# A graph propagation in dense counts: the last source tile's products of two target tiles in the two halves of the array's rows

## The reference, cut to what matters

```python
deg  = segment_sum(ones, dst);  dinv = rsqrt(max(deg, 1)) where deg > 0 else 0
norm = (dinv[src] * dinv[dst])[:, None]
def prop(h):
    return segment_sum(h[src] * norm, dst, num_segments=n)
out = gamma[0] * x
h = x
for k in range(10):
    h = prop(h)
    out = out + gamma[k + 1] * h
x = layernorm(x + out)
```

## Time and profile before

| | |
|---|---|
| median of 3 runs | 2363.64 us (2362.68 to 2366.68) |
| the profiled execution | 2366.91 us, of which 2365.2 us between the first and the last instruction |
| TensorE busy, matmul | 2159.4 us (91%), 22505 matmuls |
| TensorE busy, weight load | 1795.4 us (76%) |
| VectorE busy | 1832.0 us (77%) |
| ScalarE busy | 1162.6 us (49%) |
| propagation (first L891 to the end of its last `turn`) | 440.8 to 981.4 us |
| mean granted TensorE clock | 0.96 of full speed |

### The profile page before, as it was taken

One profiled execution on the slowest core, in us unless ns is written; L12 is line 12 of the kernel. 1 busy time (PEld: TensorE's weight loads), 2 busy tenths in 40 slices (PEclk: granted clock), 3 DMA queues, 4 the chain that ended last, 5 costly groups with the idle time before them and its releaser, 6 DMA issues. The chain is left out here.

```text
span 2365.2 us, 63175 instructions
## 1 busy us (share of the span) xinstructions
PE 2159.4 (91%) x22505; PEld 1795.4 (76%) x22506; DVE 1832.0 (77%) x2687; ACT 1162.6 (49%) x2789; POOL 879.4 (37%) x1062
## 2 busy tenths in 40 slices
PE   2888888799999999888999978999999999999897
PEld 2777777799999999622222225999996799999787
DVE  8899988765655566578999976988886788887446
ACT  1888888432332333388999966231322432230323
POOL 3444444000000000067888832555552455555000
PEclk8999999899999999989999979999998999999899
DMA  2344444200100000242222224223224322222800
GB/s 67 153 166 165 164 166 159 106 30 30 43 30 30 29 29 15 65 108 57 57 57 59 57 97 159 84 73 88 75 60 127 139 74 77 85 75 45 343 11 22
DMA packets 94785, 205.64 MB, mean 87 GB/s; under 512 B 21718, under 2 KB 61270, under 8 KB 94450
## 3 DMA queue, kind: packets, MB, share of 16 engines
q1 hardware_dynamic: 81458, 182.46, 22.3%
q0 software_dynamic: 13120, 20.18, 4.3%
HBM read 116.99 MB, written 84.76 MB: 85 GB/s over the span
## 5 line engine op out<-in xcount | busy, mean ns | idle before, releaser
L1873 PE MATMUL l_bank<-tab,mask 128*128 128x192 f16 x7600 | 636.3, 247 | 8.3 <-PEq L1704 3.5
L1873 PEld LDWEIGHTS l_bank<-tab,mask 128*128 128x128 f16 x7600 | 629.5, 98 | 10.8 <-issue 10.2
L1459 DVE TENSOR_SCALAR mask<-code 128x1600 int32<-128x1600 int32 x304 | 546.7, 1816 | 91.6 <-PE l_bank L1873 82.7
L1849 POOL DMA_INDIRECT ggot<-table_dram,gidx x408 | 386.2, 947 | 264.7 <-PE l_bank L1873 204.0
L1356 DVE TENSOR_TENSOR pr<-ex,count_copy 128x1568 f32<-128x1568 f32 x200 | 351.0, 1786 | 24.7 <-POOL ex L1255 12.8
L1346 ACT ACTIVATE ex<-score_pair,poss 128x784 f32<-128x784 f32 x400 | 344.0, 910 | 30.0 <-PE score_pair L1294 18.6
L1255 POOL TENSOR_SCALAR ex<-ex 128x1568 f32<-128x1568 f32 x200 | 298.5, 1493 | 78.2 <-ACT ex L1346 71.1
L891 PE MATMUL sums<-onehots,ct 128*128 128x192 f16 x3125 | 266.5, 250 | 11.6 <-issue 7.3
L891 PEld LDWEIGHTS sums<-onehots,ct 128*128 128x128 f16 x3125 | 263.9, 99 | 14.1 <-issue 7.9
L891 PE MATMUL sums<-u,ct 128*128 128x192 f16 x3125 | 259.1, 246 | 0.0
L891 PEld LDWEIGHTS sums<-u,ct 128*128 128x128 f16 x3125 | 258.0, 98 | 0.0
(11 more groups left out here) (344 smaller groups left out, 2873.0 us busy)
## 6 DMA issues: line engine op xcount, KB each, us to landing
code<-code_dram SPq DMA_DIRECT2D x38, 800.0 KB
code_dram<-flat SPq DMA_DIRECT2D x100, 200.0 KB, 1.9
ct_dram<-ct SPq DMA_DIRECT2D x25, 800.0 KB, 3.5
c_dram<-flat SPq DMA_DIRECT2D x25, 800.0 KB, 3.4
ct_again<-ct_dram SPq DMA_DIRECT2D x25, 800.0 KB, 17.3
cring<-c_dram SPq DMA_DIRECT2D x200, 98.0 KB, 1.9
table_dram<-tab SPq DMA_DIRECT2D x50, 384.0 KB, 2.3
flat<-code_dram SPq DMA_DIRECT2D x19, 800.0 KB, 4.4
```

The lines of the kernel that those rows point to most:

```text
L1459: e.tensor_scalar(turned.rearrange("p (s q d) -> p s q d", q=NQ, d=DQ // 2), words.rearrange("p (q s d) -> p s q d", q=NQ, d=DQ // 2), abs ...
L1849: e.indirect_dma_start(ggot[:, k, j, :], None, table_dram[:, :], bass.IndirectOffsetOnAxis(ap=gidx[:, k, j:j + 1], axis=0)).then_inc(s_ggo ...
L1873: mm = e.matmul(acc[k][:, 0:2 * D], mask[:, r % MR, s, :], tab[:, s, r, :], start=(r == 0 and s == 0), stop=(r == R - 1 and s == NT - 1))
```

## The change

In every step, target tile t now runs its 24 full products only. Behind the 24 of an odd t come two half products: source tile 24 for t - 1 from partitions 0 to 63, and source tile 24 for t from partitions 64 to 127. They use the upper and the lower half of the array's rows and write two different PSUM banks. The last tile, t = 24, has no partner and does its half alone. For this the rows 0 to 63 of `ct[:, :, 24, :]` are copied once to rows 64 to 127 by a DMA on SyncE's queue (ahead of the code loads), and the values of tile 24 are copied to partitions 64 to 127 by VectorE: once for the first step, then at the end of each step but the last. An even tile's `s_sum` is signalled behind its successor's 24 products. TensorE's wait for tile 24's values moves from the end of t = 0 to the end of t = 1; there it waits for the DMA too, and so does ScalarE before its first tile.

```diff
@@ rows_split, counting phase
                         c(e.tensor_tensor(u[0][:, ts, 1, :], val[:, ts, :], u[0][:, ts, 0, :], ALU.subtract))
+                        if ts.stop == NT:
+                            c(e.tensor_copy(u[0][HP:P, NT - 1, :, :], u[0][0:HP, NT - 1, :, :]))
@@ semaphores of the phase
+            s_twin, s_last = sem("l0_twin"), sem("l0_last")
+            assert N - (NT - 1) * P <= HP and NT % 2 == 1
@@ SyncE, behind its waits and ahead of load_code
+                    e.dma_start(ct[HP:P, :, NT - 1, :], ct[0:HP, :, NT - 1, :]).then_inc(s_twin, 16)
@@ TensorE, step
                             e.wait_ge(s_free, n + 1)
-                            for s in range(NT):
+                            for s in range(NT - 1):
                                 if t == 0:
                                     e.wait_ge(s_u, n + (s + 1))
-                                mm = e.matmul(sums[t % RS][:, 0:2 * D], ct[:, t, s, :],
-                                              u[par][:, s, :, :].rearrange("p k d -> p (k d)"),
-                                              start=(s == 0), stop=(s == NT - 1))
-                            mm.then_inc(s_sum, 1)
+                                e.matmul(sums[t % RS][:, 0:2 * D], ct[:, t, s, :],
+                                         u[par][:, s, :, :].rearrange("p k d -> p (k d)"),
+                                         start=(s == 0), stop=False)
+                            if t == 1:
+                                e.wait_ge(s_u, first + NT)
+                                e.wait_ge(s_twin, 16)
+                            if t % 2 or t == NT - 1:
+                                for v in range(t - t % 2, t + 1):
+                                    half = slice(v % 2 * HP, v % 2 * HP + HP)
+                                    e.matmul(sums[v % RS][:, 0:2 * D], ct[half, v, NT - 1, :],
+                                             u[par][half, NT - 1, :, :].rearrange("p k d -> p (k d)"),
+                                             start=False, stop=True).then_inc(s_sum, 1)
                             if last and t >= 9 and t % 5 == 4:
                                 turn(t // 5 - 1)
@@ VectorE, tile
-                            e.scalar_tensor_tensor(new[:, t, 1, :], Sb, rdeg[:, t:t + 1], new[:, t, 0, :],
-                                                   ALU.mult, ALU.subtract).then_inc(s_u, 1)
+                            low = e.scalar_tensor_tensor(new[:, t, 1, :], Sb, rdeg[:, t:t + 1], new[:, t, 0, :],
+                                                         ALU.mult, ALU.subtract)
+                            if t < NT - 1:
+                                low.then_inc(s_u, 1)
+                            else:
+                                low.then_inc(s_last, 1)
+                                e.wait_ge(s_last, k + 1)
+                                e.tensor_copy(new[HP:P, t, :, :], new[0:HP, t, :, :]).then_inc(s_u, 1)
```

## The result

The changed kernel takes **2383.05 us** (median of 4 runs, 2380.0 to 2385.2) against 2363.16 for the kernel before (4 runs, 2361.9 to 2366.7): a ratio of 1.0077 with a 95% interval of 1.0062 to 1.0092. By this ratio it is slower by 18.2 us (14.6 to 21.7); the two medians lie 19.9 us apart. The forecast was 2382.7 us, and the forecast case is the one that happened.

What follows compares the result with a forecast made beforehand. TensorE's issue pace was taken as the bound. 18.1 us for ten steps, 0.25 for the copy, 0.3 at turn(1) and 0.5 at the end gave +19.1 us, a median of 2382.7 us, range 2366 to 2392.

Steps and rivals of the forecast that it cites:

- the forecast case: Whole kernel: changes of array shape cost more than side-by-side halves save; 2382.7 us, chance 0.60.
- The bound: Propagation: TensorE's issue pace, one full product every 0.0824 us, bounds the time one for one.
- The drain: TensorE, 26 shape changes a step: each empties the array, 0.0916 us more for a change.
- The first rival: Load behind the 24th product: no drain between full and half rows; 2357 to 2359 us, chance 0.12.
- the cheaper drain: Shape changes: half rows leave sooner or only one direction drains; about 2370.7 us, chance 0.10.
- The fourth: A second cost on top: clock falls to 1.2 GHz more often, or a late DMA; 2398 us, chance 0.05.
- The halves side by side: Each pair's second half product starts 0.015 us behind the first, removing 0.067 us a pair, 8.1 us over 120 pairs.
- The sum: Propagation steps: 12 pairs and tile 24's lone half add 1.81 us a step, 18.1 us over ten steps.
- the single: Tile 24's half product without a partner, once a step: two shape changes and small sums, +0.201 us.
- The copy ahead of the barrier: End of the counting phase: VectorE's copy of tile 24's values counts whole, +0.25 us once.
- The twin DMA: Copy of ct rows ahead of the code loads: 4 us, hidden; upper bound 8 us, leaving 1 to 2 us once.
- The last step: Later tiles delay turn(1) by 0.3 us and the tail at the end by 0.5 us.

Runs made afterwards that it cites:

- e1_full_rows: Changed kernel with the last products of a pair on all 128 rows, both copies going to unread memory; 2365.05 us, 1.0012 of the kernel before.
- e4_each_half: Kernel before with the last source tile's product on rows 0 to 63 in each of 250 tiles, no pairs; 2415.37 us, ratio 1.0229.
- e2_same_half: Changed kernel with both halves of a pair on rows 0 to 63; 2389.74 us, 1.0117 of the kernel before.
- e6_last_full: Changed kernel with tile 24's last product on all 128 rows again; 2379.84 us, 1.0071 of the kernel before.
- e10_before_again: Kernel before, unedited, profiled once more; a single run of 2368.62 us.
- e5_96_rows: Kernel before with the last source tile's product on rows 0 to 95 in each of 250 tiles; 2364.70 us, ratio 1.0013.
- e8_32_rows: Kernel before with the last source tile's product on rows 0 to 31 in each of 250 tiles; 2415.20 us, ratio 1.0223.
- e7_half_stream: Kernel before with all but tile 24 in half-row products, sums not the reference's; 2361.46 us, ratio 0.9999.

## Why the prediction was right, step by step

**The bound.** TensorE's issue pace was read as the bound from the earlier trace rows. It holds: 1.8 us more in the stream of an undisturbed step, ten times, are 18 of the 18.2 us.

**The drain.** This was the step on which all hung, and its evidence was thin for rows: the earlier trace rows shows two cases at the lower clock with a semaphore near. The weight load starts 0.17 us behind the last full product, as worked out from the earlier trace rows, and 0.18 behind the halves, whose recorded time is 0.253 us instead of 0.246. That the price is a wait for the product ahead, and not a fixed price of the change, is seen where the product ahead is longer: behind the 392 columns of L1294 the load starts 1255.15 - 1254.89 = 0.26 us after its start. This is a change of columns; for rows only 192 columns were run. e1_full_rows shows that nothing else costs, e4_each_half the price by itself: 0.21 us for an excursion of two changes, where the prediction had 0.201. The first rival (no drain) and the cheaper drain fall. The fourth, a lower clock more often or a late DMA, falls too: the mean granted clock is 0.962 against 0.960, and between 440.7 and 1000 us TensorE waits for no DMA. The Trainium skill's "up to two times" stands in "TensorEngine Tiling (Array Packing)" under Overview, Theoretical Speedup, and not under Performance Considerations as the prediction has it.

**The halves side by side.** Taken as 0.015 us apart, from the earlier trace rows; at most 0.01 in the trace. 0.005 to 0.01 less, 120 times, is about 1 us that makes up for the longer way out. The outcome was right, but the row behind the 0.015 couldn't show it: L1294's two loads take 0.11 us together while their products start 0.18 apart, and e2_same_half has the same 0.11 with products that run one after the other. The four heads side by side in the columns (0.008 each) were the row that bore on it, and here the size was partly luck.

**The sum.** Pairs of +0.134 us and the single of +0.201 were to make 1.81 us a step. Measured are 1.8 for the step, 0.2 for the single (53.3 against 53.1 in e6_last_full) and so 1.6 / 12 = 0.13 for a pair.

**The copy ahead of the barrier.** 0.25 us were counted. The order of time there, as in the earlier trace rows, with the new DMA and the first pair:

```profile
439.56 0.20 DVE L505 COPY onehots<-onehots 64x192 f16<-64x192 f16 x1
440.27 0.10 POOL L872 MEMSET wmax<- 128x2 f32 x1 [18.18 <-POOLq L420]
...
440.81 0.78 SPq L850 DMA_DIRECT2D ct<-ct  x1
...
447.66 0.26 PE L906 MATMUL sums<-onehots,ct 64*128 64x192 f16 x2
```

The copy takes 0.20 us, and the barrier opens at 440.27 where it did at 440.04 (the same row in the trace of before).

**The twin DMA.** It was taken at 4 us, hidden. Its row in the list of DMA issues between 440 and 446 us (the last number is us from issue to landing):

```profile
ct<-ct SPq DMA_DIRECT2D x1, 400.0 KB, 4.7
```

It landed at 440.8 + 4.7 = 445.5, 2.2 us before the first pair at 447.66 asks for it. The issue of the two code loads behind it took 2.7 us instead of 1.0, which nobody waited for.

**The last step.** 0.3 us were put at turn(1) and 0.5 at the end. Around turn(1):

```profile
964.66 0.26 PE L906 MATMUL sums<-u,ct 64*128 64x192 f16 x2
...
965.80 1.29 DVE L994 TENSOR_SCALAR x<-x,l_st 128x96 f32<-128x96 f32 x5
...
967.14 0.75 PE L887 MATMUL ln_turned<-ident,x 128*96 128x128 f32 x5
```

The turn starts 2.48 us behind the pair. The norm ends at 967.09, and the 24 products that start at 964.85 would have been followed at 964.85 + 24 x 0.0824 = 966.83: a wait of 0.3 us, as worked out. At the end, the last product and the last turn of after, then the last turn of before:

```profile
989.68 0.25 PE L906 MATMUL sums<-u,ct 64*128 64x192 f16 x1
...
996.51 1.30 PE L887 MATMUL ln_turned<-ident,x 128*96 128x128 f32 x5 [5.88 <-DVE x L994]
```
```profile
980.07 1.30 PE L881 MATMUL ln_turned<-ident,x 128*96 128x128 f32 x5 [5.65 <-DVE x L974]
```

From the last product to the last turn are 996.51 - 989.68 = 6.8 us, and were 980.07 - 973.6 = 6.5 before: 0.3 to 0.4 us more, where 0.5 was put. Beside the 0.3 us at turn(1) no wait of TensorE for VectorE was added within the steps: the others are three gaps at the loop turns in both profiles (6.3 us now, 7.3 before).

**Where the profile and the medians part.** The profiled execution grew by 14.8 us (2366.9 to 2381.7), the median by 19.9. The propagation grew by 16.2 us in it, and two things that the change doesn't touch were shorter. The gathering phase took 723.5 us where it had 726.3. And one stretch at 1.2 GHz behind a loop turn is missing, in step 4: its clock is 1.00 here and was 0.97 before. Step 4 of after, then of before:

```profile
662.80:717.00 54.20, 54.16 (x626) 50.42 (x627) 29.40 (x78) 16.20 (x40) 0.00 (x0) 1.00 0.10 32
```
```profile
656.30:710.10 53.80, 53.79 (x626) 53.13 (x627) 30.05 (x78) 16.42 (x40) 0.00 (x0) 0.97 0.10 32
```

It grew by 0.4 us only, 1.4 less than step 8. Against a step of the kernel before that has full clock too, step 2 of e10_before_again, it is 1.8 us longer:

```profile
547.70:600.10 52.40, 52.40 (x625) 51.81 (x626) 30.03 (x78) 16.43 (x40) 0.00 (x0) 1.00 0.10 33
```

The missing stretch makes the 16.2 up to 17.6, near the 18 or so of ten steps and the edges. The forecast for the profiled execution (2386.0) was thus 4.3 high and that for the median 0.35 low; such closeness of the latter is partly luck, as the interval of 7 us says.

## What to carry to other kernels

Before packing a few small products side by side, count the changes of the array's shape, not the products: here each excursion cost 0.21 us, more than two full products of 192 columns, and saved one. Read the price from a place in the trace where the shape already changes: in this kernel the load behind it starts some 0.07 us before the modelled end of the matmul ahead, instead of beside it. Where packing is wanted, make it the rule for the whole stream and the full shape the exception, and then look again at what the other engines do in the new rhythm.

## What the runs showed of the hardware beyond the forecast

- Shapes of 96 and 128 rows mix almost freely (e5_96_rows, 0.1 us a step), shapes of 64 and of 32 rows behind 128 cost the same 0.21 us an excursion (e4_each_half, e8_32_rows).
- A stream of nothing but half products in two row halves starts a pair every 0.083 us, with two loads and two matmuls each (e7_half_stream); the doubled number of instructions cost nothing.
- Two half products from the same rows start 0.09 us apart right behind a change of shape (e2_same_half), from different rows at most 0.01.
